# Seven block products per pair of tiles: from three PSUM banks and summed parts to two banks and copied partial sums

## The reference, cut to what matters

```python
masked_w = weight * mask                                   # (8, 512, 512)
w_bot = einsum('bg,got->bot', cond_8, masked_w)            # one 512x512 matrix per batch
h = einsum('bnt,bot->bno', x, w_bot) + bias                # (2, 2048, 512), fp32

def bitlinear(x, w):                                       # x to 8 bits per row, w to -1, 0, 1
    return einsum('bsi,oi->bso', act_quant(x), weight_quant(w))

p = silu(bitlinear(h, w_gate)) * bitlinear(h, w_up)        # (2, 2048, 2048)
out = x + bitlinear(p, w_down)                             # 2048 -> 512
```

## Time and profile before

| | us |
|---|---|
| median of three runs | 464.94 (463.86 to 465.05) |
| the profiled execution | 464.25 |
| its span, first to last instruction | 462.4 |
| TensorE busy in the span | 444.5 (96%) |
| VectorE busy | 338.7 (73%) |
| ScalarE busy | 288.7 (62%) |
| GpSimd busy | 156.8 (34%) |

### The profile page before, as it was taken

How to read it: one execution, slowest core, us unless ns; L and a number is a source line. 1 busy time by engine, 2 the same in 40 slices (tenths; PEclk the granted TensorE clock), 3 DMA queues, 4 the chain that set the end, 5 groups by cost and what they waited for, 6 DMA issues and landing times.

```text
span 462.4 us, 7082 instructions
## 1 busy us (share of the span) xinstructions
PE 444.5 (96%) x2184; PEld 236.2 (51%) x2222; DVE 338.7 (73%) x587; ACT 288.7 (62%) x381; POOL 156.8 (34%) x175
## 2 busy tenths in 40 slices
PE   4899999999999899999999999999999999999995
PEld 0234443444444355555555565565656555555562
DVE  0326779898956778787877878778787877878693
ACT  1216767775346767666676766667676676766660
POOL 0000251505291005342433524244352423524263
PEclk9999999999999999999999999999999999999999
DMA  8999996986212324554625345352544624245464
GB/s 283 404 403 412 411 234 154 378 229 146 48 35 43 71 47 102 128 117 107 127 63 136 85 105 132 87 136 45 136 105 105 139 61 136 68 114 127 102 138 136
DMA packets 104312, 69.77 MB, mean 151 GB/s; under 512 B 87264, under 2 KB 87264, under 8 KB 102752
## 3 DMA queue, kind: packets, MB, share of 16 engines
q1 hardware_dynamic: 103712, 67.39, 53.8%
q10 hardware_dynamic: 576, 2.10, 1.3%
HBM read 40.11 MB, written 8.39 MB: 105 GB/s over the span
## 4 chain that ended last, share of the span: by engine, by line
PE 73%; DMA 10%; SPq 6%; ACT 4%; DVE 3%; issue 3%; DVEq 0%; ACTq 0%
PE ps L690 46%; PE ps L709 19%; PE ps L659 8%; DMA wc<-w_gate 4%; DMA qT<-q_sb 3%; DMA wc<-w_down 2%; SPq L189 2%; SPq L182 1%; SPq L185 1%; ACT tern_up L353 1%; SPq L193 1%; ACT h_sb L359 1%; PE ps L717 1%; DMA wc<-wc 1%; ACT q_sb L364 1%
## 5 line engine op out<-in xcount | busy, mean ns | idle before, releaser
L375 ACT ACTIVATE wc<-ps,gate_unit 128x512 f32<-128x512 f32 x128 | 88.0, 689 | 97.6 <-PE ps L690 87.1
L570 DVE TENSOR_TENSOR wc<-ps,wc 128x512 f32<-128x512 f32 x128 | 88.4, 692 | 63.2 <-PE ps L690 46.0
L690 PE MATMUL ps<-tern_up,qT 128*128 128x512 bf16 x509 | 130.7, 379 | 0.2
L690 PE MATMUL ps<-tern_gate,qT 128*128 128x512 bf16 x477 | 126.1, 379 | 3.9 <-DVE wc L570 2.0
L659 PE MATMUL ps<-w_bot,xT_sb 128*128 128x512 f32 x256 | 113.2, 595 | 2.3 <-DVE w_bot L475 1.6
L690 PEld LDWEIGHTS ps<-tern_up,qT 128*128 (+1 forms) x512 | 50.1, 98 | 60.4
L575 DVE TENSOR_REDUCE p_part<-wc 128x1 f32<-128x1536 f32 x64 | 78.1, 1220 | 2.2
L659 PEld LDWEIGHTS ps<-w_bot,xT_sb 128*128 128x128 f32 x256 | 48.0, 190 | 61.3 <-issue 57.5
L690 PEld LDWEIGHTS ps<-tern_gate,qT 128*128 (+1 forms) x512 | 49.9, 98 | 44.6 <-issue 5.9
L389 ACT ACTIVATE wc<-wc 128x1024 f16<-128x1024 f32 x64 | 64.5, 1064 | 0.7 <-DVE wc L613 0.6
L709 PE MATMUL ps<-wc 128*128 128x256 f16 x480 | 62.2, 273 | 0.0
(11 more groups left out here) (63 smaller groups left out, 308.8 us busy)
## 6 DMA issues: line engine op xcount, KB each, us to landing
xT_sb<-xT SPq DMA_DIRECT2D x32, 256.0 KB, 6.8
x_res<-x SPq DMA_DIRECT2D x30, 256.0 KB, 2.8
out<-result SPq DMA_DIRECT2D x30, 256.0 KB, 2.2
wc<-wcond SPq DMA_DIRECT2D x12, 512.0 KB, 13.5
wc<-w_gate SPq DMA_DIRECT2D x4, 1024.0 KB, 17.3
wc<-w_up SPq DMA_DIRECT2D x4, 1024.0 KB, 12.2
wc<-w_down SPq DMA_DIRECT2D x4, 1024.0 KB, 7.6
wc<-wcond ACTq DMA_DIRECT2D x4, 512.0 KB, 7.6
```

The lines of the kernel that those rows point to most:

```text
L375: nc.scalar.activation(silu[:, c % 2], ps[:, GATE + c % 2], ACT.Silu, scale=unit).then_inc(silu_ready, 1)
L570: nc.vector.tensor_tensor(prod[:, par, 512 * c:512 * c + 512], ps[:, UP + c % 2], silu[:, c % 2], ALU.mult).then_inc(prod_ready, 1)
L690: ins = nc.tensor.matmul(ps[:, bank + c % 2], tile, w[:, c, k], start=(k == 0), stop=(k == KH - 1))
```

## The change

Block products: two banks, A and B, take the place of X, Z and V. The order of the seven is new. Product 0 (first in the odd step) now needs the block sum 0 (`qsum[0]`, second tile of the pair, both halves). ScalarE copies bank A to SBUF (`copy_shared`) after product 0 and bank A to bank B (`copy_seed`) after product 1, and writes three of the four result blocks scaled to `result` (`scale_c11`, `scale_c12`, `scale_c21`). VectorE writes A plus the copy into B after product 3 (`sum_seed`), and A plus the copy to `result` after product 5 (`sum_c22`). GpSimd scales one block (`scale_c22`) and adds the residual for each tile in one operation of 512 (`finish_first`, `finish_second`).

Conversion to f16: the first half of each tile stays on ScalarE, the second goes to GpSimd (`convert_second`).

Condition products of tiles 30 and 31: over steps 0 to 2 at eight places, with their VectorE and ScalarE work in steps 2 and 3. The block sum 0 is moved to the head of the odd step on VectorE. SyncE issues the two stores of a pair together, ahead of the transposes of the odd step's tile. The unpaired products of tiles 30 and 31 are cut into halves and put between block products.

The core of the diff:

```diff
 # TensorE
+LATE_SLICES = {(0, 1): (0, 0), (0, 3): (0, 1), (1, 0): (0, 2), (1, 1): (0, 3), (1, 3): (1, 0), (2, 0): (1, 1),
+               (2, 1): (1, 2), (2, 2): (1, 3)}
             def down_product(j, i, b0, b1):
-                if i < 3 and not first:
-                    pe.wait_ge((c11_done, c21_done, c12_done)[i], j)
-                if i < 2:
-                    pe.wait_ge(s_q2T[i], 32 * j + 16 + 16 * i)
-                if i >= 3:
-                    pe.wait_ge(part_out, 4 * j + i - 2)
-                if i in (2, 4, 5, 6):
-                    pe.wait_ge(sum_ready, 4 * j + (0, 0, 1, 0, 2, 3, 4)[i])
-                bank = (X, Z, V, X, Z, V, Z)[i]
+                if i == 0 and not first:
+                    pe.wait_ge(c21_out, j)
+                if i == 1:
+                    pe.wait_ge(shared_copied, j + 1)
+                if i == 2:
+                    pe.wait_ge(seed_copied, j + 1)
+                if i == 4:
+                    pe.wait_ge(seed_summed, j + 1)
+                if i == 6:
+                    pe.wait_ge(c22_done, j + 1)
+                if i in (1, 2):
+                    pe.wait_ge(s_q2T[i - 1], 32 * j + 16)
+                if i == 6:
+                    pe.wait_ge(s_q2T[1], 32 * j + 32)
+                if i in (0, 3, 4, 5):
+                    pe.wait_ge(sum_ready, 4 * j + (1, 0, 0, 2, 3, 4)[i])
+                bank = (A, A, B, A, B, A, A)[i]
...
 # TensorE, the end
             down_product(PAIRS - 1, 3, b0, b0 + 1)
+            for half in range(2):
+                down_plain(LATE, half)
             down_product(PAIRS - 1, 4, b0, b0 + 1)
-            down_plain(LATE, LAST)
             down_product(PAIRS - 1, 5, b0, b0 + 1)
+            down_plain(LATE + 1, 0)
             down_product(PAIRS - 1, 6, b0, b0 + 1)
-            pe.wait_ge(c11_done, PAIRS)
-            down_plain(LATE + 1, X)
+            down_plain(LATE + 1, 1)
 # GpSimd
             for t in range(TILES):
+                if t >= 5 and t % 2 == 1:
+                    finish_second((t - 5) // 2)
+                if t > 0:
+                    convert_second(t - 1)
+                if t >= 4 and t % 2 == 0:
+                    finish_first((t - 4) // 2)
+                    scale_c22((t - 4) // 2)
                 unit_of(t)
-                if t == LATE + 1:
-                    join_parts(PAIRS - 1)
-                elif t >= 3 and t % 2 == 1:
-                    join_parts((t - 3) // 2)
-                elif t >= 4:
-                    finish_pair((t - 4) // 2)
-            finish_pair(PAIRS - 1)
+            convert_second(TILES - 1)
+            finish_first(PAIRS - 1)
+            scale_c22(PAIRS - 1)
+            finish_second(PAIRS - 1)
 # GpSimd: what finish_second and convert_second are
+                pool.wait_ge(c21_out, j + 1)
+                pool.wait_ge(c22_scaled, j + 1)
+                pool.wait_ge(s_xres[1], 16 * j + 16)
+                nc.gpsimd.tensor_tensor(result[:, 1], result[:, 1], x_res[:, 1], ALU.add).then_inc(result_ready, 1)
...
+                pool.wait_ge(p_rounded, t + 1)
...
+                nc.gpsimd.tensor_scalar(q2[:, 1024:2048], prod[:, t % 2, 1024:2048], -ROUND, 0.0, ALU.add, ALU.add
+                                        ).then_inc(q2_ready[1], 1)
 # ScalarE, odd step (the even one: scale_c11 first, scale_c12 behind round_tile)
+                if s >= 5:
+                    scale_c21(j - 1)
                 silu_chunk(s, 0)
+                silu_chunk(s, 1)
+                round_tile(s - 1, 0)
+                if j is not None:
+                    copy_shared(j)
+                silu_chunk(s, 2)
+                convert_first(s - 1)
+                if j is not None:
+                    copy_seed(j)
+                silu_chunk(s, 3)
 # VectorE
             def step(s, par, late=None, j=None, b0=0):
+                if j is not None and par == 1:
+                    add_blocks(j, 0, b0, b1)
                 product(s, par, 0)
-                if j is not None and par == 1 and not (isinstance(j, int) and j == 0):
-                    join_blocks(j - 1)
                 if j is not None and par == 0:
+                    sum_seed(j)
                     add_blocks(j, 3, b0, b1)
                 product(s, par, 1)
                 if late is not None:
                     cond_tile(late)
                 if j is not None and par == 1:
-                    add_blocks(j, 0, b0, b1)
                     add_blocks(j, 1, b0, b1)
                 if j is not None and par == 0:
                     add_blocks(j, 2, b0, b1)
-                    finish_c11(j, s - 4)
                 product(s, par, 2)
+                if j is not None and par == 0:
+                    sum_c22(j)
                 largest(s, par, 0, 0, 3)
                 product(s, par, 3)
                 largest(s, par, 1, 3, 4)
```

More of the change, by code:

```diff
@@ L161, in build @@
         s_last = sem("s_last")
-        q2_ready = sem("q2_ready")
+        q2_ready = [sem(f"q2_ready{i}") for i in range(2)]
         down_psum = sem("down_psum")
@@ L254, in _ @@
                     store(s - 5)
+                    store(s - 4)
                 transpose_q2(s - 1)
[L256 to L259, removed]
+                if s in (2, 3):
+                    transpose_q(LATE + s - 2)
                 if s == 4:
@@ L398, in step, with copy_shared @@
[L398 to L401, removed]
-                silu_chunk(s, 0)
-                if even is not None:
-                    copy_part(even, 1)
+                    act.wait_ge(s_q2T[0], 16 * t)
+                nc.scalar.activation(q2[:, 0:1024], prod[:, t % 2, 0:1024], ACT.Copy, bias=-ROUND).then_inc(q2_ready[0], 1)
+            def copy_shared(j):
+                act.wait_ge(down_psum, 7 * j + 1)
+                if j > 0:
+                    act.wait_ge(c22_done, j)
+                nc.scalar.activation(shared, ps[:, A, 0:NB], ACT.Copy).then_inc(shared_copied, 1)
@@ L405, in step, with even_step @@
+            def even_step(s):
+                j = (s - 4) // 2 if s >= 4 else None
+                if j is not None:
+                    scale_c11(j)
+                silu_chunk(s, 0)
                 silu_chunk(s, 1)
                 if s > 0:
[L407 to L411, removed]
+                    round_tile(s - 1, 1)
+                if j is not None:
+                    scale_c12(j)
@@ L412, in step @@
                 silu_chunk(s, 2)
-                if even is not None:
-                    copy_part(even, 3)
                 if s > 0:
[L416 to L419, removed]
+                    convert_first(s - 1)
                 silu_chunk(s, 3)
+                if s == 2:
+                    cond_round(LATE)
             for i in range(4):
@@ L438, in _ @@
                     abs_sum_piece(*abs_after[t])
[L439 to L444, removed]
+            for s in range(0, TILES, 2):
+                even_step(s)
+                odd_step(s + 1)
+            scale_c11(PAIRS - 1)
+            convert_first(TILES - 1)
+            scale_c12(PAIRS - 1)
+            scale_c21(PAIRS - 1)
         @block.vector
@@ L720, in _, with down_plain @@
+                ins.then_inc(down_psum, 1)
+            def down_plain(t, half):
+                pe.wait_ge(s_q2T[half], 16 * t + 16)
+                for k in range(KB * half, KB * half + KB):
+                    ins = nc.tensor.matmul(ps[:, LAST[t - LATE]], q2T[:, t % QBUF, k], tern_down[:, k], start=(k == 0),
+                                           stop=(k == KI - 1))
+                if half == 1:
+                    ins.then_inc(plain_psum, 1)
             pe.wait_ge(mix_w_ready, 3)
```

188 lines of the change are left out of this document (93 added, 95 removed).

## The result

| | before | after |
|---|---|---|
| median of four runs each, us | 464.54 (463.86 to 465.05) | 467.94 (467.55 to 468.37) |
| the profiled execution, us | 464.25 | 468.27 |
| its span, us | 462.4 | 466.5 |

The ratio is 1.0074, with a 95% interval from 1.0055 to 1.0093: the change costs 3.4 us. The sign and the range of the prediction held, its size didn't: it had put the change at 472.1, 7.2 us above the 464.94 of before that it started from (7.6 above the median in this table), more than twice as much.

A forecast was written before the change was run, and what follows sets the result against it. TensorE was taken as the bound, busy 39.74 of 40.00 us in the loop. 464.25 - 0.8 (start) + 7.8 (late product 0) + 0.5 (end) = 471.8, put at 472.1 us with half of a 0.7 offset; range 463.2 to 475.5.

The forecast's parts named there:

- product 0 is late in every pair: Head of the odd step: the block sum 0 waits for GpSimd's `finish_second`, so product 0 starts 0.56 us late.
- the lock: VectorE's block sum and GpSimd's addition exclude each other; the first to issue holds the shared ports for its whole instruction.
- 1 (GpSimd second): Before product 0: the block sum runs first and GpSimd's addition waits; 464.0 us, no change; chance 0.20.
- 2 (a short wait, or product 4 late): In the loop: product 0 0.12 late, or product 4 0.1 to 0.2; 465.6 to 467.5 us; chance 0.14 with the fourth rival.
- 3 (the start gives all): Second stage's start: both waits of steps 2 and 3 gone, no loop loss; 462.0 us; chance 0.11.
- 4 (`sum_c22` doesn't shift VectorE): Even step: GpSimd starts 0.3 earlier, product 0 is 0.24 late; 467.4 us; chance 0.14 with the second rival.
- the term 14 x 0.56 = 7.8 us: Loop: product 0's delay of 0.56 us, counted for the 14 pairs with a `finish_second` ahead of them.
- the conversion's price: GpSimd's conversion of 1024 columns to f16: taken as 1.1 us, between 1.07 and 2.13.
- The cover named for it: GpSimd's conversion can begin at 253.8; its transpose can't be issued before the first half's at about 257.
- Start and end: Outside the loop: 0.8 us gained at the start (0 to 2.3), 0.5 lost at the end (-0.3 to +1.5).

The follow-up runs named there:

- e2_convert_scalar: The changed kernel with both halves of each tile converted on ScalarE, none on GpSimd: 467.27 us, ratio 1.0055 to the kernel before.
- e4_fast_form: The changed kernel with GpSimd's conversion written as multiply, add rather than add, add (1.04 us instead of 3.63): 467.99 us, ratio 1.0077 to the kernel before.
- e1_second_early: The changed kernel with GpSimd's `finish_second` ahead of `unit_of` rather than behind it: 465.42 us, ratio 1.0017 to the kernel before.
- e8_split_add: The changed kernel with all conversions on ScalarE and `finish_second` issued as two additions of 256 columns: 462.56 us, ratio 0.9969 to the kernel before.

## Why the prediction was right in its mechanism and wrong in its size

**Right: product 0 is late in every pair, because the block sum waits for GpSimd's addition.** Place, cause and count held: rows of the change show it, e2_convert_scalar and e4_fast_form show that the landing doesn't matter while the lock stands, e1_second_early and e8_split_add take the lock away in two ways and the loss goes with it. None of the rivals occurred. 1 (GpSimd second): in e4_fast_form the addition starts 0.49 ahead of the sum, not 0.28. 2 (a short wait, or product 4 late): the sum waits until the addition is done in all 14 pairs, and in the loop TensorE doesn't wait for product 4. 3 (the start gives all) needed rival 1. 4 (`sum_c22` doesn't shift VectorE): it does, the long maximum starts 5.41 us ahead of product 0's due time in e4_fast_form (236.08 against 241.49), before 5.93 (255.45 against 261.38). That the time came out next to the 467.4 of rival 4 is chance.

**Wrong, and the step that failed: the term 14 x 0.56 = 7.8 us.** It measures 14 x 0.33 = 4.6 us. e4_fast_form has the priced conversion, so the 0.23 can be split there and in the change. First, the addition starts 1.54 us ahead of product 0's due time (239.95 against 241.49), not 1.41. I took 1.87 from the start of the long maximum to the next product from the earlier trace rows, but that product had a wait of its own in it (chunk 3's up products, of the kernel before, end at 246.82, the product starts at 246.92). Where VectorE isn't made to wait, the distance is 1.66 (257.04 to 258.70 below), 0.21 less. Against this `sum_c22` came 0.11 later than I had it: it starts 0.13 behind the end of product 5 (235.74 against 234.57 + 1.04 in e4_fast_form), where I had taken 0.03. The steps from that product to the addition are 0.03 shorter together. 0.21 - 0.11 + 0.03 = 0.13. The row of before, and the rows of the change:

```profile
245.79 1.03 PE L690 MATMUL ps<-tern_up,qT 128*128 128x512 bf16 x4
```

```profile
256.70 0.42 DVE L587 TENSOR_TENSOR result<-ps,w_bot 128x256 f32<-128x256 f32 x1 [0.19 <-PE ps L750]
257.04 1.74 DVE L607 TENSOR_REDUCE p_part<-wc 128x1 f32<-128x1536 f32 x1
...
258.70 0.68 DVE L602 TENSOR_TENSOR wc<-ps,wc 128x512 f32<-128x512 f32 x1
```

Second, from the sum's end to product 0 it is 0.05 to 0.06 us (242.47 to 242.52; 241.76 to 241.82), not the 0.15 of the earlier trace rows. 0.13 and 0.10 make the 0.23, and 14 x 0.23 = 3.2 us is most of the miss (471.8 had been put for the profiled execution, 468.27 was measured, 3.5 us; the end makes 0.8 more of it, the start 0.5 less): in a difference of two long chains each tenth counts fourteen times.

**Wrong, but it didn't decide: the conversion's price.** 1.07 to 2.13 us had been the bounds, 3.63 is the measured time. The cover named for it (up to the second transpose) wasn't enough: the sum's earliest start came 0.4 later than in e4_fast_form (0.96 against 1.38 ahead of product 0). It cost 0.8 at the start, product 0 of step 3; in the loop the lock hid it.

**Start and end.** From the first chunk of the stage to chunk 0 of step 5 the change takes 49.28 us, before 49.84: 0.56 gained where 0.8 was forecast, the first product 0 being 1.1 late and product 4 only 0.1 (the rows are of the change; the kernel before has 178.22, and 128.38, which is worked out: the first record is missing, the row begins at 128.59).

```profile
128.64 1.03 PE L723 MATMUL ps<-tern_gate,qT 128*128 128x512 bf16 x4
...
177.92 1.03 PE L723 MATMUL ps<-tern_gate,qT 128*128 128x512 bf16 x4
...
461.23 1.90 PE L757 MATMUL ps<-tern_down,wc 128*128 128x512 f16 x8 [0.72 <-DMA wc<-wc]
...
462.78 1.50 SPq L271 DMA_DIRECT2D out<-h_sb  x2
463.17 0.75 DVE L593 SCALAR_TENSOR_TENSOR h_sb<-ps,out_unit,q_sb 128x512 f32<-128x512 f32 x1 [4.17 <-PE ps L757]
```

The same of the kernel before, chunk 0 of step 5 and VectorE's last operation:

```profile
178.22 1.03 PE L690 MATMUL ps<-tern_gate,qT 128*128 128x512 bf16 x4
...
457.81 0.75 DVE L562 SCALAR_TENSOR_TENSOR h_sb<-ps,out_unit,q_sb 128x512 f32<-128x512 f32 x1 [2.37 <-PE ps L717]
```

(The stage itself began 0.26 later in this execution.) At the end the last products finish 1.0 later relative to their order, but the last store is now issued as soon as VectorE has ended (463.92), while before it stood in SyncE's queue until 459.4, 0.9 behind VectorE's end at 458.56; and it lands 2.0 us after its issue, before 2.5. So the end as a whole, from product 0 of the last pair to the last instruction, is 0.3 shorter (21.4 us, before 21.7) rather than 0.5 longer. 4.6 - 0.56 + 0.26 - 0.3 = 4.0, the difference of the two spans (4.1 by the rounded values of the table).

**Right: nothing else in the loop waits.** In the change TensorE has no idle time there but the one before product 0. `shared_copied`, `seed_summed` and `c22_done` were in time; ScalarE's copy from PSUM to PSUM took 0.37, inside its bounds, VectorE's sum into PSUM 0.43.

## What to carry to other kernels

Where TensorE sets the pace, rate a reordering by its tightest new chain, and ask for each VectorE operation with two SBUF inputs on that chain what GpSimd has just begun: issue the GpSimd operation earlier, or cut it in two. When a price is taken from a neighbouring row, take the same pair of operations, not the same engine and size; and take spacings between instructions only from places where neither was waiting. Before shortening an operation, see which wait ends last: 2.6 us off each conversion was worth nothing with the lock in place and 3 us in all without it.

## What the runs showed of the hardware that I had not expected

On GpSimd 1024 columns of fp32 take 3.63 us with add, add and 2.77 with a single add, but 1.04 with multiply by 1.0 and add, and 1.04 as a plain conversion; where both outputs, f16 and fp32, were measured (add and add, multiply by a column and add, plain), the type made no difference above 0.01 us. A VectorE block sum that meets a GpSimd addition ended 0.55 us behind it in every case (1.27 us or 0.72 us long), and a GpSimd addition of 0.72 that meets the sum takes 1.18.

GpSimd's conversion holds a block sum up too, but not for its whole length in the slow form. It shows before product 4 of the last pair, where the conversion of the last tile has just begun, first in the change (3.63 us), then in e4_fast_form (1.04 us); each row of VectorE has two sums, of which the first takes 1.42 and the second 0.68:

```profile
454.24 3.63 POOL L328 TENSOR_SCALAR wc<-wc 128x1024 f16<-128x1024 f32 x1 [1.49 <-DVE wc L646]
454.40 2.02 DVE L574 TENSOR_TENSOR wc<-wc 128x1024 f16<-128x1024 f16 x2
...
455.97 1.03 PE L750 MATMUL ps<-tern_down,wc 128*128 128x256 f16 x8 [0.36 <-DVE wc L574]
```

```profile
453.52 1.04 POOL L328 TENSOR_SCALAR wc<-wc 128x1024 f16<-128x1024 f32 x1 [1.48 <-DVE wc L646]
453.68 2.02 DVE L574 TENSOR_TENSOR wc<-wc 128x1024 f16<-128x1024 f16 x2
...
455.25 1.03 PE L750 MATMUL ps<-tern_down,wc 128*128 128x256 f16 x8 [0.35 <-DVE wc L574]
```

In both the first sum ends 1.58 us after the conversion's start, so the long form holds it up no longer than the short one, and the second sum of the change runs at 0.68 beside the rest of it. Why the long form lets go early is open.
